# A two-layer graph network on one core: the destinations' inverse root degrees by one-hot products instead of table gathers, scatters issued before the power, ScalarE's steps reordered

## The reference

```python
h  = relu(layernorm(x))
x1 = x + gnn0(h)          # layer 0
# gnn0: z = layernorm(h)*g + b;  q = z Wq + bq, k, v likewise
#       dk = silu(attr Wdk + bdk), dv likewise
#       a = silu(sum(q[dst] * k[src] * dk)) * cosine_cutoff(ew)
#       agg = segment_sum(v[src] * dv * a, dst);  gnn0 = h + agg Wo + bo
h1 = relu(layernorm(x1))
x2 = x1 + gnn1(h1)        # layer 1
# gnn1: deg = 1 + segment_sum(ew, src);  dinv = rsqrt(deg)
#       agg[src] += dinv[src] * ew * dinv[dst] * (h1 W)[dst], plus self loops dinv^2 * (h1 W)
#       gnn1 = relu((agg + b) W1 + b1) W2 + b2
```

## Time and profile before

| | |
|---|---|
| runs (us) | 2002.97, 2006.59, 2006.33; median 2006.33 |
| profiled execution | 2008.08, its span 2006.4 |
| busy (us) | PE 1598.3, PEld 1047.8, DVE 1343.3, ACT 1188.1, POOL 1343.7 |
| DMA | 391.94 MB, 195 GB/s over the span |
| granted TensorE clock | mean 0.888 |

### The profile page before, as it was taken

How to read it: one execution, slowest core, us unless ns; L and a number is a source line. 1 busy time by engine, 2 the same in 40 slices (tenths; PEclk the granted TensorE clock), 3 DMA queues, 4 the chain that set the end, 5 groups by cost and what they waited for, 6 DMA issues and landing times.

```text
span 2006.4 us, 30280 instructions
## 1 busy us (share of the span) xinstructions
PE 1598.3 (80%) x6241; PEld 1047.8 (52%) x6241; DVE 1343.3 (67%) x5623; ACT 1188.1 (59%) x2271; POOL 1343.7 (67%) x996
## 2 busy tenths in 40 slices
PE   5917989898989898254445424999999999999999
PEld 2304555555555555133333313666767666666766
DVE  7945656665666664555455538788888888888883
ACT  5914555554555554122221226888989898989984
POOL 2044788888888885688888876566666666666660
PEclk9958999999999999666665656999999999999999
DMA  7995555555555556354454568899999999999981
GB/s 246 418 353 198 154 161 160 152 142 155 162 160 148 145 156 172 78 88 88 88 91 84 88 124 212 248 254 265 275 269 273 266 273 264 272 270 267 274 254 70
DMA packets 153340, 391.94 MB, mean 195 GB/s; under 512 B 24660, under 2 KB 68796, under 8 KB 153292
## 3 DMA queue, kind: packets, MB, share of 16 engines
q1 hardware_dynamic: 88844, 258.08, 38.1%
q0 software_dynamic: 59552, 115.52, 30.9%
q10 hardware_dynamic: 4896, 17.83, 2.3%
HBM read 211.36 MB, written 179.98 MB: 195 GB/s over the span
## 4 chain that ended last, share of the span: by engine, by line
PE 38%; DMA 18%; POOL 17%; issue 12%; ACT 7%; DVE 6%; ACTq 1%; SPq 1%; DVEq 0%; POOLq 0%
PE bank L1381 15%; PE bank L1370 15%; DMA sums_dram<-ub,sidx 7%; POOL cg L487 6%; DMA kept<-in_x_dram,look 5%; POOL sums_dram L483 5%; PE bank L1360 4%; PE bank L1221 3%; DMA cg<-sums_dram,ic 3%; ACT z L1068 2%; POOL kept L487 1%; DVE cg L875 1%; POOL tab_d L487 1%; DVE st L737 1%; POOL kept L569 1%
## 5 line engine op out<-in xcount | busy, mean ns | idle before, releaser
L483 POOL DMA_INDIRECT sums_dram<-ub,sidx x196 | 317.8, 1622 | 84.0 <-issue 43.5
L1370 PE MATMUL bank<-kept,w 128*128 128x512 f32 x784 | 355.8, 597 | 0.0
L569 POOL TENSOR_TENSOR kept<-kept 128x1024 f32<-128x1024 f32 x98 | 233.6, 2383 | 182.2 <-DVE cg L952 182.2
L1381 PE MATMUL bank<-w_sb,kept 128*128 128x256 f32 x1568 | 354.3, 379 | 0.0
L1381 PEld LDWEIGHTS bank<-w_sb,kept 128*128 128x128 f32 x1568 | 297.9, 190 | 81.9 <-issue 46.4
L1335 PE MATMUL bank<-cg,en 128*128 128x256 f32 x392 | 173.1, 619 | 204.7 <-ACT cg L1126 199.7
L1280 PE MATMUL bank<-qkv_w,zT 128*128 128x512 f32 x392 | 210.4, 662 | 80.6 <-ACT zT L1038 80.5
L1335 PEld LDWEIGHTS bank<-cg,en 128*128 128x128 f32 x392 | 117.8, 314 | 259.7 <-issue 235.2
L479 POOL TENSOR_TENSOR b_rs<-b_ve,minus_half 128x8 f32<-128x8 f32 x102 | 210.2, 2061 | 24.1 <-DVE b_ve L969 24.1
L1370 PEld LDWEIGHTS bank<-kept,w 128*128 128x128 f32 x784 | 142.8, 192 | 142.6 <-issue 142.5
L1147 ACT ACTIVATE kept<-kept,b_nb,b_rs 128x256 f32<-128x256 f32 x392 | 202.2, 589 | 16.6 <-DVE b_nb L942 16.6
(11 more groups left out here) (185 smaller groups left out, 3198.7 us busy)
## 6 DMA issues: line engine op xcount, KB each, us to landing
sums_dram<-cg SPq DMA_DIRECT2D x162, 512.0 KB, 13.3
kept<-in_x_dram SPq DMA_DIRECT2D x97, 512.0 KB, 5.5
kept<-sums_dram POOLq DMA_DIRECT2D x97, 512.0 KB, 9.9
cg<-sums_dram SPq DMA_DIRECT2D x97, 512.0 KB, 8.6
out_dram<-cg SPq DMA_DIRECT2D x97, 512.0 KB, 9.7
sums_dram<-cg ACTq DMA_DIRECT2D x34, 512.0 KB, 6.3
row_d<-in_dst_dram SPq DMA_DIRECT2D x48, 128.0 KB, 3.5
row_s<-in_src_dram SPq DMA_DIRECT2D x48, 128.0 KB, 3.3
```

Of the source, the lines that this page charges most:

```text
L483: pool.indirect_dma_start(sums, bass.IndirectOffsetOnAxis(idx, 0), rows, None, bounds_check=last_row, compute_op=ALU.add).then_inc(done, 16)
L569: pool.tensor_tensor(X1[k.slot(8)], X[k.slot(4)], H[k.slot(2)], ALU.add).then_inc(g_xh, 1)
L1370: ins = pe.matmul(bank[:, 2 + m, :], w01[:, c, m * P:(m + 1) * P], hT[k.slot(2)][:, c * GN:(c + 1) * GN], start=(c == 0), stop=(c == KC - 1))
L1381: ins = pe.matmul(to, rT[k.slot(2)][:, c * GN + j * P:c * GN + (j + 1) * P], w2_sb[:, c, :], start=False, stop=(c == KC - 1), skip_group_c ...
```

## The change

- `dinv` is no longer stored to DRAM as a table, and the 98 one-number gathers `tab_d` (two a pair in GpSimd's message step) are gone.
- Instead, SP stores the destinations' partition keys once (`keys`, 50 KB), and in the edge stage loads them for each pair as a row of 256 on all partitions (`row_k`, 128 KB). VectorE compares that row with the partition number (`HT`, one-hot, transposed). TensorE multiplies HT by `dinv` (128 x 392), which gives each edge the whole table row of its destination in PSUM (banks 2 to 5). One step later VectorE picks the column by comparing a column count with ckey, multiplying and summing (`found`), and makes the norm of the pair.
- GpSimd's message step now has the scatters of pair p-7 ahead of the power of pair p-2.
- ScalarE's message step is now: turned(0), UB, silu_d(0), turned(1), scaled(0), scaled(1), silu_d(1), Relus, ST, sa.
- GpSimd's `messages2` is unrolled with constants, and its gathers read node indices directly; VectorE's copies `ic` and their waits are gone.
- VectorE waits for all fills ahead of the edge stage, since `picked` reuses their buffers.

```diff
-            sp.wait_ge(s_tab_sb, 1)
-            sp.dma_start(table.rearrange("(p c) k -> p (c k)", p=P), dinv[:, :]).then_inc(s_table, 16)
+            sp.wait_ge(s_key, 1)
+            sp.dma_start(keys.rearrange("(c p) -> c p", p=P), e_keyf[:, :]).then_inc(s_keys, 16)
...                                                            # SP load_src
+                    if k.past(2):
+                        pass_on(sp, (n_ht, k.value(-1)))
+                    elif not k.past(1):
+                        sp.wait_ge(s_keys, 16)
+                    sp.dma_start(row_k[k.slot(2)][:, :],
+                                 keys[bass.ds(k.value(0, 2 * P), 2 * P)].rearrange("(a e) -> a e", a=1)
+                                 .broadcast_to([P, 2 * P])).then_inc(n_key[k.slot(2)], 16)
...                                                            # GpSimd messages(p)
                 if p < EP:
                     gather_x(p)
+                k = p - 7
+                if 0 <= k < EP:
+                    pool.wait_ge(m_UB, k + 1)
+                    pool.wait_ge(m_idx, k + 1)
+                    if k >= 1:
+                        pool.wait_ge(m_sc, 32 * k)
+                    else:
+                        pool.wait_ge(s_fill, 16 * (NG + 1))
+                    for i in range(2):
+                        scatter_add(sums0, sidx[:, 2 * k + i:2 * k + i + 1], UB[2 * (k % 2) + i], m_sc)
                 k = p - 2
...                                                            # the power of pair p-2, as before
-                k = p - 1
-                if 0 <= k < EP:
-                    if k == 0:
-                        pool.wait_ge(s_table, 16)
-                    for i in (2 * k, 2 * k + 1):
-                        gather(tab_d[:, i, :], table, look[:, i, 2:3], last_entry, m_tab)
-                k = p - 7                                       # the scatters, now above
...                                                            # GpSimd messages2, unrolled
+                p = s.off
+                if p < EP:
+                    if p >= 2:
+                        pool.wait_ge(n_x1, p - 1)
+                    for i in range(2):
+                        gather(C0[p % 2][:, i, :], sums0, node_i[:, 2 * p + i, 0:1], last_row, n_c0[p % 2])
...                                                            # VectorE setup
+            link(dve.tensor_scalar(e_key[:, :], e_rows[:, 1, :].bitcast(I32), 2, P - 1, ALU.logical_shift_right,
+                                   ALU.bitwise_and))
+            dve.tensor_copy(e_keyf[:, :], e_key[:, :]).then_inc(s_key, 1)
+            link(dve.tensor_scalar(part_f[:, :], dump_f[:, 0:1], float(-N), None, ALU.add))
...                                                            # VectorE ahead of messages2
-            dve.wait_ge(m_tab, 16 * EC)
-            link(dve.tensor_tensor(norm[:, :], tab_d[:, :, 0], ew_f[:, :], ALU.mult))
+            dve.wait_ge(s_fill, 16 * (NG + 1))
+            dve.wait_ge(s_fill1, 16 * NG)
...                                                            # VectorE messages2, after nb
+                    dve.wait_ge(n_key[q], k.turns(2))
+                    if k.past(2):
+                        dve.wait_ge(n_look, k.value(-1))
+                    dve.tensor_scalar(HT[q][:, :], row_k[q][:, :], part_f[:, 0:1], None, ALU.is_equal).then_inc(n_ht, 1)
...                                                            # pair a = s-1, ahead of X1e
+                    dve.wait_ge(n_look, a.value(1))
+                    for i in range(2):
+                        ins = dve.scalar_tensor_tensor(
+                            picked[2 * q + i], iota_c[:, :],
+                            ckey[:, bass.ds(a.value(0, 2) + i, 1), 0], bank[:, 2 + 2 * q + i, 0:COLS],
+                            ALU.is_equal, ALU.mult, accum_out=found[:, bass.ds(a.value(0, 2) + i, 1)])
+                    ins.then_inc(n_sel, 1)
...                                                            # after the statistics
+                    dve.wait_ge(n_sel, a.value(1))
+                    dve.tensor_tensor(cols(norm, a), cols(found, a), cols(ew_f, a), ALU.mult).then_inc(n_norm, 1)
...                                                            # ScalarE messages
-                if s.back(3).within(EP):
-                    scaled(0)
                 if s.back(4).within(EP):
                     turned(1)
                 if s.back(3).within(EP):
+                    scaled(0)
                     scaled(1)
+                if s.back(4).within(EP):
+                    silu_d(1)
...                                                            # the Relus; silu_d(1) was behind them
-                if s.back(4).within(EP):
-                    silu_d(1)
...                                                            # TensorE messages2, ahead of the product with EN
+                k = s
+                q = k.slot(2)
+                if k.within(EP):
+                    if not k.past(1):
+                        for done, n in ((m_msg, EC), (m_at, EC), (m_ST, EP)):
+                            pe.wait_ge(done, n)
+                    pe.wait_ge(n_ht, k.value(1))
+                    if k.past(2):
+                        pe.wait_ge(n_sel, k.value(-1))
+                    for i in range(2):
+                        ins = pe.matmul(bank[:, 2 + 2 * q + i, 0:COLS], HT[q][:, i * P:(i + 1) * P], dinv[:, :],
+                                        start=True, stop=True)
+                    ins.then_inc(n_look, 1)
```

More of the change, by code:

```diff
@@ L178, in build @@
         pkey = temp([P, EC, 2])
-        ckey = temp([P, EC, 2])
+        ckey = sb("ckey", [P, EC, 2])
+        part_f = sb("part_f", [P, 1])
         valid = sb("valid", [P, EC])
@@ L278, in build @@
         sidx2 = ring("sidx2_", 4, [P, 2], I32)
-        ic = ring("ic_", 2, [P, 2], I32)
+        row_k = ring("row_k_", 2, [P, 2 * P])
+        HT = ring("ht_", 2, [P, 2 * P])
+        found = sb("found", [P, EC])
+        picked = [CG[0].rearrange("p a d -> p (a d)")[:, i * COLS:(i + 1) * COLS] for i in range(4)]
         row_s = ring("row_s_", 2, [P, 2 * P], I32)
@@ L534, in messages2 @@
             def messages2(s):
[L535 to L541, removed]
[L542 to L555 removed]
+                p = s.off
+                if p < EP:
+                    if p >= 2:
+                        pool.wait_ge(n_x1, p - 1)
+                    for i in range(2):
+                        gather(C0[p % 2][:, i, :], sums0, node_i[:, 2 * p + i, 0:1], last_row, n_c0[p % 2])
+                k = p - 1
+                if 0 <= k < EP:
+                    inv_sqrt(ve[k % 2][:, :, :], rs[k % 2][:, :, :], n_ve, n_rs, s.back(1))
+                k = p - 5
+                if 0 <= k < EP:
+                    pool.wait_ge(n_UB, k + 1)
+                    pool.wait_ge(n_idx, k + 1)
+                    if k >= 1:
+                        pool.wait_ge(n_sc, 32 * k)
+                    else:
+                        pool.wait_ge(s_fill1, 16 * NG)
                     for i in range(2):
[L557 to L559 removed]
+                        scatter_add(sums1, sidx2[k % 4][:, i:i + 1], UB[2 * (k % 2) + i], n_sc)
+            for p in range(EP + 1):
+                messages2(Step(p))
             def nodes(s):
@@ L899, in messages2 @@
                         dve.wait_ge(n_U, a.value(-1))
+                    dve.wait_ge(n_norm, a.value(1))
                     for i in range(2):
@@ L915, in messages2 @@
                                       ALU.add).then_inc(n_idx, 1)
-                k = s.back(-1)
-                if k.within(EP):
-                    if k.past(2):
-                        pass_on(dve, (n_c0[k.slot(2)], k.back(2).turns(2, 32)))
-                    ends(k)
             run_steps(dve, EP, 1, 4, PAIR_STEPS + 3, messages2)
@@ L1341, in open_banks @@
             def open_banks():
-                for done, n in ((m_at, EC), (m_ST, EP), (m_UB, EP), (m_zT, EC)):
+                for done, n in ((m_at, EC), (m_ST, EP), (m_UB, EP), (m_zT, EC), (n_sel, EP)):
                     pe.wait_ge(done, n)
```

57 lines of the change are left out of this document (20 added, 37 removed).

## The result

The changed kernel takes 1926.88 us (median of 4 runs, 1925.64 to 1931.16), the kernel before, run beside it, 2004.65 (2002.54 to 2006.59): ratio 0.9616, 95% interval 0.9597 to 0.9635. The profiled execution took 1926.92 us, span 1925.3. The forecast was 1909, range 1893 to 1944.

The account below looks back on a forecast made before the run. GpSimd's queue was taken to bound the message stage (13.1 us a pair) and the edge stage. Terms -87.6 - 10 - 1 - 2.4 - 2 + 5 + 0.5 = -97.5 on 2008.08 gave 1910.6, 1909 for the median; range 1893 to 1944.

Parts of the forecast that it names:

- Message stage: Pairs 4 to 48: without table gathers TensorE becomes the bound, 11.05 us a pair for 13.04, gaining 87.6 us.
- rival A: Message stage: the power's new place, not TensorE, sets the step; 12.2 us a pair, 51 us more, 1960; chance 0.14.
- ScalarE's order: Message stage: the zT copy no longer waits behind scaling; losing this costs 1.9 us waiting, up to 1.6 slower matmuls a step.
- Start: Start of the message stage: third pair's gathers no longer wait for the table store; 10 us gained (bounds 4 and 17).
- tail: End of the message stage: scatters ahead of the power start the last chain earlier; 2.4 us gained (0 to 8).
- the edge stage's first pairs: First four pairs, bound by the VectorE-power-VectorE loop: added VectorE work is not covered, costing 5 us (2 to 8).
- Edge stage, steady part: Second layer's edge stage, 43 pairs: GpSimd stays the bound, 7.40 us a pair for 7.44; -2 us (bounds -6 and +28).
- SyncE loads one more row of 128 KB a pair, asked for almost two steps ahead: hidden: Edge stage: the added key row load was taken to cost no time.
- The price that I had set beside the sum for GpSimd's scatters: Edge stage: VectorE's comparison might lengthen one more scatter issue by 0.09 us, making the sum 4 us higher.
- Rival B: Edge stage: the lookup loop decides at 1.2 GHz, 8.0 us a pair, 29 us more, 1938; chance 0.16.
- Node stage: Node stage, 1200 to 1950 us: DMA at 0.96, taken as not touched by the change; no term in the sum.
- My own signs of being wrong: TensorE idling for z, message step over 11.5 us, EN waiting over 2 for the aggregation, or edge scatter spacing over 7.8.

Follow-up runs that it names:

- e7: The kernel before without the table gathers, both old orders kept, no lookup and no root degree in the second layer's norm; 1918.64 us, ratio 0.9576.
- e3: The changed kernel with ScalarE's old order (first scaling ahead of the second zT copy, second Silu behind the Relus); 1931.05 us, ratio 0.9636.
- e1: The changed kernel with the key row loaded for the first two pairs only and reused; 1927.79 us, ratio 0.9597.
- g1: The kernel of e1 again, on another occasion; 1911.65 us, ratio 0.9505.
- f1: The changed kernel with the keys as bytes, loaded for all pairs by one DMA after the message stage's loads; 1910.71 us, ratio 0.9501.
- e8: The kernel before with one more 128 KB broadcast row load a pair in the edge stage, read by nobody; 2094.47 us, ratio 1.0423.
- f0: The changed kernel with one VectorE memset of a spare column behind the edge stage, a probe of repeatability; 1935.17 us, ratio 0.9618.
- e2: The changed kernel without TensorE's lookup products and VectorE's picks, row loads and comparison kept; 1960.01 us, ratio 0.9748.
- e6: The kernel before with both new orders (scatters ahead of the power, ScalarE's steps), table gathers kept, no lookup; 2022.95 us, ratio 1.0087.
- f2: The kernel of f1 with only two source row loads as well, pairs reusing the first two pairs' sources; 1899.37 us, ratio 0.9447.

## Why the prediction was right, and where it was not

- Message stage: right in bound and size. TensorE sets it at 10.98 us (forecast 11.05), and rival A fell: the power waits at most 0.6 us for its variance. e7 shows that taking out the gathers does most of it, with 11.26 us in the old orders. What I held of ScalarE's order, that without its cover each step could lose over 2 us, was too dear: e3 lost 1.4 us in 44 steps, and both old orders together 12.
- Start, tail and the edge stage's first pairs: -8.6, -2.2 and +3.8 for -10.5, -2.4 and +5. The start gained less because the first Relu came 1.15 us later, where I had 0.5 for the setup, and because ScalarE's fills took longer to issue than before, 1.44 us each instead of 1.30 in the run of seven.
- Edge stage, steady part: the step that failed is "SyncE loads one more row of 128 KB a pair, asked for almost two steps ahead: hidden". Hidden it was for its reader. But it travels beside the scatters, whose landing closes the loop: 6.46 us became 7.00, and over 7.7 in 7 of 43 steps. e1, g1 and f1 show it by taking the load away, e8 by putting one in. Of the 0.54 us a pair 0.40 is this load (7.98 - 7.58), 17 of 23 us, and 0.57 on f0's chip; the other 0.14 is the lookup or the unrolled list, which I have not separated. How the load delays a landing, I have not shown.
- The price that I had set beside the sum for GpSimd's scatters, 0.09 us more for one issue, did not come: they take 1.64 us after as before, in the rows above and in the earlier trace rows.
- Rival B had the size, 8.0 us a pair, by another cause. Without the lookup e2 stays at 8.22, with it f1 has 7.58. Its weak point was the clock, which didn't stay at 0.61. The granted clock over 250 us of the edge stage was 0.79 in the changed kernel and 0.62 in e2, which differs by the lookup:

```profile
823.20:1073.20 250.00, 147.03 (x377) 92.05 (x375) 157.99 (x717) 48.76 (x93) 193.66 (x156) 0.79 0.51 98
```
```profile
850.80:1100.80 250.00, 112.88 (x247) 77.08 (x245) 124.23 (x581) 47.15 (x90) 187.08 (x152) 0.62 0.50 95
```

The rule that I had cited from the Trainium skill (TensorE: Matmul & The Clock Gate, What's actually happening), that activity releases the clock, agrees with these rows. The clock rose to 0.79, though, and not to the message stage's level: my argument set these bursts beside a stage in which TensorE was busy 489 of 552 us, and here it is busy 147 of 250.

- Node stage: 6.5 us, not forecast at all. VectorE stood still once in the kernel before, with nothing in the trace that it waited for, behind the entry to its node loop:

```profile
1289.79 1.67 DVE L980 SCALAR_TENSOR_TENSOR kept<-cg,dinv,kept 128x256 f32<-128x256 f32 x4
1297.38 0.16 DVE L939 TENSOR_TENSOR b_rs<-b_rs,dinv 128x4 f32<-128x4 f32 x1 [5.91 <-issue]
```

The changed kernel has no such wait. Over all 14 profiles the five whose VectorE code lacks the lookup's picks (before, e2, e6, e7, e8) have it, 5.4 to 6.1 us, and take 808.6 to 811.3 us from the last pair's first scatter to the end; the nine with the picks don't, and take 802.0 to 806.2. So it goes with the code that stands ahead of the loop; why was not tried by itself. The Trainium skill (Runtime: NRT & Kernel Launch, Instruction fetch mechanics) says that a taken branch to code outside the loaded blocks has to wait for its fetch; the rows fit that, and show no more than the wait.

- My own signs of being wrong came true for the edge stage: the scatters' spacing was to stay below 7.8 us and was 7.98, and EN's waits for the aggregation reached 2.8 us where I had set 2 (they average 1.6 in 22 waits between 770 and 1050 us).

The total came out 18 us above the forecast as the sum of unlike errors: 25 us too good in the edge stage, 6.5 too bad in the node stage, up to 3 elsewhere. It would have stayed in the range without the luck of the node stage, at 1933. But the range reached that far because of rival B's 8.0 us a pair, so it covered a cost whose cause, the landing, I had not named.

## What to carry to other kernels

A transfer that comes early enough for its reader can still be on the path, through the transfers that it delays: where a chain of scatters closes over its own landing, ask of each added load what is in flight when it goes out, and load once for all steps what is small (here 24.5 us, f0 to f1). When an engine's list of work explains a stage's step, look also for what its waits end with; two loops 0.1 us apart give the same step until one of them is stretched. And compare variants stage by stage: one kernel came out 0.9% apart on two occasions, far outside each interval.

## What the runs showed of the hardware

- One broadcast row load of 128 KB (256 words to 128 partitions) that leaves 2 to 3.5 us behind a pair's first scatter-add lengthens the time to the pair's landing: 6.46 us with one (6.73 to 6.76 in the kernels with the lookup), 7.00 with two that leave 0.67 us apart, 8.67 in e8 with two 0.43 us apart, the unread row first. With none it was 5.80 (f2, which scatters to other rows as well). With half of the bytes in the second one it was 6.91, not clearly less than 7.00.
- From the landing of a scatter to the start of the next one that waits for it: medians of 0.83 to 0.86 us in thirteen profiles.
- The same instruction list at the same TensorE start times had its results seen by ScalarE 1.0 us later on one chip than on another (e1 and the changed kernel, ds at 215.52 and 214.50), with the message stage 16 us longer; open.
- VectorE stood still for 5.4 to 6.1 us once, behind the entry to its node loop and with no releaser in the trace, in five kernels, and not in nine whose code ahead of that loop was longer.
